# A transform of 64 by 32 points with half-array matmuls, and two bias rows added by matmul

## The reference

```python
# block 1: Hyena operator, order 2
proj = (layernorm(x) @ in_proj_w + in_proj_b).reshape(B, L, C, 3)
v = depthwise_conv3(proj[..., 0]) + short_b
h = gelu(gelu(pos @ fw1 + fb1) @ fw2 + fb2)
coefs = (h @ fw3 + fb3).reshape(L, C, 2)
for i in range(2):                       # only i = 1 reaches the output
    conv = irfft(rfft(v, 2L) * rfft(coefs[..., i], 2L), 2L)[:, :L]
    output = proj[..., i + 1] * conv
x = x + output @ out_w + out_b
# block 2: a weighted sum of 8 chosen adapters, one 512x512 matrix W and one bias b
x = x + layernorm(x) @ W.T + b
```

## Time and profile before

| | us |
|---|---|
| median of 3 runs (lowest, highest) | 2708.38 (2707.97, 2709.68) |
| span of the profiled execution; no other time of it is given | 2708.2 |
| busy: TensorE, VectorE, GpSimd, ScalarE | 2570.4, 1723.3, 1304.6, 1289.9 |

### The profile page before, as it was taken

One profiled execution on the slowest core, in us unless ns is written; L12 is line 12 of the kernel. 1 busy time (PEld: TensorE's weight loads), 2 busy tenths in 40 slices (PEclk: granted clock), 3 DMA queues, 4 the chain that ended last, 5 costly groups with the idle time before them and its releaser, 6 DMA issues. The chain is left out here.

```text
span 2708.2 us, 38386 instructions
## 1 busy us (share of the span) xinstructions
PE 2570.4 (95%) x11252; PEld 1859.0 (69%) x11252; DVE 1723.3 (64%) x2429; ACT 1289.9 (48%) x2021; POOL 1304.6 (48%) x1446
## 2 busy tenths in 40 slices
PE   7679999999999999799999997899999999999999
PEld 2268888888888888433333332788888888888887
DVE  5834434343443434477777776788888888888886
ACT  6634444444444444599999997222222222222222
POOL 1422222222222222366666664676767767776775
PEclk8889999999999999999999999999999999999999
DMA  6533443444344343777777776665555555555553
GB/s 207 171 121 117 183 167 132 158 155 159 119 180 170 128 164 139 263 248 259 263 254 252 249 252 227 233 212 171 169 165 170 170 161 172 169 165 170 169 166 124
DMA packets 233303, 495.89 MB, mean 183 GB/s; under 512 B 20299, under 2 KB 37004, under 8 KB 220244
## 3 DMA queue, kind: packets, MB, share of 16 engines
q1 hardware_dynamic: 181012, 394.39, 43.4%
q10 hardware_dynamic: 52224, 100.68, 9.9%
HBM read 275.58 MB, written 219.43 MB: 183 GB/s over the span
## 5 line engine op out<-in xcount | busy, mean ns | idle before, releaser
L1114 POOL TENSOR_TENSOR m_m<-m_zs,m_spec 128x512 f32<-128x512 f32 x256 | 345.2, 1353 | 240.7 <-ACT m_zs L1070 218.0
L776 POOL TENSOR_TENSOR vl<-v,vh 128x512 fp32r<-128x512 f32 x128 | 165.3, 1291 | 469.7 <-ACT vh L728 469.7
L1029 PE MATMUL m_psW<-m_u,mats 128*128 128x512 f32 x512 | 283.4, 636 | 48.8 <-DVE m_u L1143 48.1
L1143 DVE TENSOR_TENSOR m_u<-m_m 128x512 f32<-128x512 f32 x256 | 269.4, 1062 | 90.2 <-POOL m_m L1114 51.2
L1070 ACT ACTIVATE m_zs<-m_psZ 64x512 f32<-64x512 f32 x512 | 302.5, 591 | 22.1 <-DVE m_m L1131 9.1
L880 DVE COPY fs1o<-psS 128x512 f32<-128x512 f32 x128 | 88.5, 691 | 334.6 <-PE psS L201 334.6
L1305 ACT ACTIVATE b_z<-b_y,b_shift,b_rstd 128x512 f32<-128x512 f32 x128 | 104.3, 815 | 376.0 <-POOL b_shift L1269 376.0
L728 ACT ACTIVATE vh<-v 128x512 fp32r<-128x512 f32 x128 | 80.9, 632 | 401.7 <-DVE v L859 401.7
L1330 PEld LDWEIGHTS b_psC<-b_s,b_fin 128*128 128x128 f32 x2048 | 249.9, 193 | 23.6 <-DMA b_fin<-spec 12.9
L1330 PE MATMUL b_psC<-b_s,b_fin 128*128 128x128 f32 x2048 | 250.9, 276 | 12.5 <-DMA b_fin<-spec 12.5
L1018 PE MATMUL m_psZ<-m_xin,mats 128*128 128x512 f32 x512 | 256.7, 594 | 0.0
(11 more groups left out here) (128 smaller groups left out, 5894.4 us busy)
## 6 DMA issues: line engine op xcount, KB each, us to landing
m_xin<-spec SPq DMA_DIRECT2D x31, 2304.0 KB, 13.2
spec<-fs1o SPq DMA_DIRECT2D x64, 1024.0 KB, 5.8
spec<-m_wo ACTq DMA_DIRECT2D x64, 1024.0 KB, 7.0
b_fin<-spec SPq DMA_DIRECT2D x128, 512.0 KB, 3.7
xg<-in_L_attn_x_dram SPq DMA_DIRECT2D x32, 1024.0 KB, 4.8
gate_t<-gto SPq DMA_DIRECT2D x32, 1024.0 KB, 4.3
b_gin<-gate_t SPq DMA_DIRECT2D x128, 256.0 KB, 3.6
b_xin<-in_L_attn_x_dram SPq DMA_DIRECT2D x128, 256.0 KB, 3.8
```

The lines of the kernel that those rows point to most:

```text
L776: pool.tensor_tensor(vl[:, t % 2], v[:, t % 2], vh[:, t % 2].bitcast(F32), ALU.subtract).then_inc(v_lo, 1)
L1029: pe.matmul(psW[k][:], kind(INV, i, t), u[:, (t % GB - 1) % R, :], start=True, stop=True).then_inc(w_ps, 1)
L1114: pool.tensor_tensor(m2[:, b % R, :], zs[:, b % R, :], spec[:, par, 1, :], ALU.mult).then_inc(m2_done, 1)
L1143: dve.tensor_tensor(u[:, b % R, :], m1[:, b % R, :], m2[:, b % R, :], ALU.add).then_inc(u_done, 1)
```

## The change

All of the transform goes over to 64 by 32 points: 64 slots of spectrum instead of 128 and 32 inner indices. A tile is now two inner indices, t and t + 16, of 64 rows each (h = 0, 1), in partitions 0 to 63 and 64 to 127; there are 16 tiles per batch as before (`T`). The transform steps become pairs of matmuls on half of the array, without tile positions being named: they follow from the partitions of the operands.

- `prep`: filter rows, running sums and first transform in pairs; the channel-major filter, its copies, three scans and the rearrangements go; the sum runs over the hidden layer (one scan), and a second matmul chain (`sums`) turns it into edge rows.
- `front`: `stage1` has six matmuls on 64 rows each; the gate is projected row-major tile by tile (`project_g`), its bias added by VectorE; one copy of both banks on ScalarE.
- `middle`: weights hold each matrix beside its swapped form, so that a pair of row halves gives both parts of the product; one VectorE product of 1024 columns; the inverse is a pair of column halves and adds the two parts; swap, GpSimd's product and the sum go.
- `back`: `conv` is a pair of column halves with row-major result; `turn_o` transposes the gated rows; both bias rows enter as a first matmul on 64 rows in `project` and `adapt`; `bias_x` and `bias_y` go; lags and orders change.

```diff
 # front, TensorE
-                    for j in range(2):
-                        mm = mm3(pe, psS[j][:], s1h[:, t, j * P:(j + 1) * P], s1l[:, t, j * P:(j + 1) * P],
-                                 vh[:, t % 2], vl[:, t % 2], True, True)
+                    lo, hi = slice(0, N1), slice(N1, P)
+                    for half, h in ((lo, 0), (hi, 1)):
+                        pe.matmul(psS[:, h, :], s1h[half, t, :], vh[half, t % 2, :], start=True, stop=False)
+                    for half, h in ((lo, 0), (hi, 1)):
+                        pe.matmul(psS[:, h, :], s1h[half, t, :], vl[half, t % 2, :], start=False, stop=False)
+                    for half, h in ((lo, 0), (hi, 1)):
+                        mm = pe.matmul(psS[:, h, :], s1l[half, t, :], vh[half, t % 2, :], start=False, stop=True)
...
-                pipelined(pe, B, N2, [(turn, 2), (project_v, 3), (project_x2, 6), (stage1, 4)])
+                pipelined(pe, B, T, [(turn, 2), (project_v, 3), (project_g, 3), (stage1, 4)])
 # middle, TensorE
+            PAIR_AT = {0: 0, 2: 1, 4: 2, 7: 3}
...
-                    pe.matmul(psZ[(t % GB - 1) % R][:], kind(FWD, i, t), xin[:, par, t % GB - 1, :],
-                              start=True, stop=True).then_inc(z_ps, 1)
+                    pe.matmul(psA[k % RA][:, 0, :], w[0:R2], src[0:R2], start=True, stop=True)
+                    mm = pe.matmul(psA[k % RA][:, 1, :], w[R2:P], src[R2:P], start=True, stop=True)
...
-                    pe.matmul(psW[k][:], kind(INV, i, t), u[:, (t % GB - 1) % R, :], start=True, stop=True).then_inc(w_ps, 1)
+                    for k in range(2):
+                        pe.wait_ge(m_done, n + k + 1)
+                        pe.matmul(psW[0:R2, k, :], back_first if first else back_w, m[:, (2 * pair + k) % RM, 0, :], start=True, stop=True)
+                        pe.matmul(psW[R2:P, k, :], back_w, m[:, (2 * pair + k) % RM, 1, :], start=True, stop=True).then_inc(w_ps, 1)
 # middle, VectorE
+                    dve.tensor_tensor(m[:, (k - 1) % RM], psA[k % RA][:], spec[:, par], ALU.mult).then_inc(m_done, 1)
 # back, TensorE
-                    for ct in range(CT):
-                        for j in range(2):
-                            mm = pe.matmul(psC[t % 2][:, ct * P:(ct + 1) * P], fin[:, t % 2, j, ct * P:(ct + 1) * P],
-                                           s4[:, j, t, :], start=(j == 0), stop=(j == 1))
+                    for h in range(2):
+                        mm = pe.matmul(psC[t % 2][h * N1:(h + 1) * N1, :], s4[:, h * T + t, :], fin[:, t % 2, h, :], start=True, stop=True)
+                def turn_o(b, t):
+                    pe.wait_ge(o_done, no(b, t) + 1)
...
+                        mm = pe.transpose(psP[:, ct * P:(ct + 1) * P], o[:, t % 2, ct * P:(ct + 1) * P], ident[:])
                 def project(b, t):
...
+                    pe.matmul(psO[t % 2][:], share_r[:], bohl[:], start=True, stop=False)
...
                 def adapt(b, t):
...
+                    pe.matmul(psF[t % 2][:], share_r[:], bfhl[:], start=True, stop=False)
...
-                pipelined(pe, B, N2, [(conv, 1), (project, 2), (turn, 3), (adapt, 4)])
+                pipelined(pe, B, T, [(conv, 1), (adapt, 4), (turn_z, 3), (turn_o, 1), (project, 2)])
 # prep, TensorE: filter_rows, and sums likewise with cum and ramp_r
-                        pe.matmul(pA[e % 2][:], h2[:, cols], w3s[:], start=True, stop=False)
+                    for h in range(2):
+                        cols = h2[:, e + h * T:e + h * T + (N1 - 1) * N2 + 1:N2]
+                        pe.matmul(pA[e % 2][h * N1:(h + 1) * N1, :], cols, w3s[:], start=True, stop=False)
+                    pe.matmul(pA[e % 2][:], inside_r[:, where], b3hl[:], start=False, stop=True).then_inc(H_ps, 1)
```

More of the change, by code:

```diff
@@ L347, in _ @@
+                for i in range(4):
+                    sp.wait_ge(e0_stored[i], 16 * T // 4)
+                for i in range(3):
+                    sp.wait_ge(e1_stored[i], 16 * len(range(i, T, 3)))
+                sp.wait_ge(consts_in, 32)
                 sp.wait_ge(fc["x_in"][0], 16)
@@ new lines, in sums, with stage1 @@
+                def sums(t):
+                    if t >= 2:
+                        pe.wait_ge(e1_done, t - 1)
+                    for h in range(2):
+                        cols = cum[:, t + h * T:t + h * T + (N1 - 1) * N2 + 1:N2]
+                        pe.matmul(pE[t % 2][h * N1:(h + 1) * N1, :], cols, w3s[:], start=True, stop=False)
+                    pe.matmul(pE[t % 2][:], ramp_r[:, t * P:(t + 1) * P], b3hl[:], start=False, stop=True).then_inc(c_ps, 1)
+                def stage1(t):
+                    edge_row = t == T - 1
+                    pe.wait_ge(g_done, t + 1)
+                    if t >= 2:
+                        pe.wait_ge(s1_out, t - 1)
+                    for h in range(2):
+                        half = slice(h * N1, (h + 1) * N1)
+                        end = not (edge_row and h == 1)
+                        mm = pe.matmul(pS[t % 2][:, h, :], s1[half, t, :], g[half, t % GR, :], start=True, stop=end)
+                    if edge_row:
+                        pe.wait_ge(before_done, 1)
+                        mm = pe.matmul(pS[t % 2][:, 1, :], s1x[:], g_before[:], start=False, stop=True)
+                    mm.then_inc(s1_ps, 1)
@@ L501, in _ @@
+                for e in range(T + LAG):
+                    if e < T + 2:
+                        filter_rows(e)
+                    if e == 0:
+                        pe.wait_ge(cum_done, 1)
+                    if e < T:
+                        sums(e)
                     if e == LAG:
@@ L1145, in _ @@
-                pipelined(dve, GROUPS // 2, T, [(same_part, 0), (product, 2)])
+                    par, k = s // GB, s % GB
+                    n = data_no(i, s)
+                    dve.wait_ge(a_ps, n + 1)
+                    if k == 1:
+                        dve.wait_ge(f_done, group(i, s) + 1)
+                    if not (at_first(i, s) and k <= RM):
+                        dve.wait_ge(w_ps, n - RM + 1)
+                    dve.tensor_tensor(m[:, (k - 1) % RM], psA[k % RA][:], spec[:, par], ALU.mult).then_inc(m_done, 1)
```

833 lines of the change are left out of this document (352 added, 481 removed).

## The result

The changed kernel takes 3200.58 us (median of 4 runs, 3197.47 to 3203.96), the kernel before 2709.03 beside it: a ratio of 1.1816, 95% interval [1.1799, 1.1832]. Predicted were 2894 us and a range that ended at 3140. The direction was right; the size was not, and neither was the reason. The profiled execution spans 3202.1 us.

The account below looks back on a forecast made before the run. TensorE was taken to bound front and back, and a loop of ScalarE, VectorE and GpSimd middle. The sum was 2708 - 12 (prep) - 39 (front) + 60 (middle) + 177 (back) = 2894 us, range 2630 to 3140.

Parts of the forecast that it names:

- Prep, -12: Prep: copies, rearrangements and three scans go, half-array pairs come; 112 to 130 us against 137.8, taken as -12 us.
- Front, -39: Front: six whole matmuls become three pairs and two mode changes, -0.31 us a tile over 128 tiles, -39 us.
- Middle, +60: Middle: TensorE becomes the bound with 17 pairs, late second halves and mode changes; 19.6 us per group, 627 us, +60.
- but in program order: Fp32 pairs: the second half's first record starts only with the first half's second, so n pairs take 0.86 n + 0.43 us.
- rival 1: Whole kernel: pairs overlap wholly, mode changes still cost 0.19 us; middle -51, back +122, total 2728 us; chance 0.13.
- The term of 0.43 per run: Middle: a late second half at the end of each of eight runs per group, 8 x 0.43 = 3.4 us.
- Back, +177: Back: TensorE's tile goes from 7.81 to 9.19 us with bias matmuls, transposes and five mode changes, +177 us.
- The relief: Back: the two additions on VectorE and GpSimd were hidden by slack, so removing them brings nothing.
- the lower bound by the loop: Back: the chain from projection through y, statistics and z to the next projection needs 8.1 us per tile, +37 us.
- the late second halves: Middle and back: second halves start late; 0.43 us per run in middle, a lone pair in back 1.29 us, not 0.86.

Follow-up runs that it names:

- e_before_share: Kernel before with back's two bias additions replaced by matmuls over 64 rows, transform and transfers as before; 2861.20 us, ratio 1.0562.
- e_back16: Changed kernel with back's load of x and store of the output written as two transfers each, one per half; 2755.79 us, ratio 1.0177.
- e_adds16: Changed kernel with back's x load and output store in two transfers each, and both bias rows added by additions again; 2742.19 us, ratio 1.0116.
- e_turnz_rows128: Changed kernel with back's transfers split in two, bias matmuls on 128 rows, and z's transpose between adapter and projection; 2660.60 us, ratio 0.9817.
- e_adds: Changed kernel with both bias rows of back added by additions again, x's first in VectorE's order, slow transfers kept; 3317.44 us, ratio 1.2249.
- e_before2: Kernel before with back's x load and output store taken as a pattern of 2 x 64 rows; 3306.30 us, ratio 1.2205.
- e_x16: Changed kernel with back's load of x alone written as two transfers, the output store left as it was; 2775.58 us, ratio 1.0247.
- e_adds_late: Changed kernel with bias additions and slow transfers, b_out added to x right ahead of the addition that needs it; 3198.83 us, ratio 1.1815.

## Why the prediction was wrong

- **Prep, -12.** Too much: the first transpose of front starts at 144.3 us, for 143.8. In the other kernels with this prep it starts between 138.8 and 145.1, so the gain is 5 us at most and in most traces less. TensorE has 4 us less to do, but waits for `e`, which VectorE makes (21.5 us in ten waits), and VectorE for the store of `e` (12.4). Which of these sets the part was not tested.
- **Front, -39.** Right: its last stage-1 product starts at 1058.0 for 1095.4 us, 37 less; the tile is 7.07 us by its transposes (144.3 to 1042.8 over 127), for 7.09 predicted. With 0.23 for a pair of fp32r halves and 0.19 for a change the sum holds.
- **Middle, +60.** Wrong by its sign: -43 by the windows (524 for 567). The step was "but in program order": the second half's first record was to wait for the first half's second. It doesn't; pairs start 0.01 us apart. Without that term the same sum is rival 1's 516 us, and the first forward to the last inverse takes 515.9 (1071.3 to 1587.2). The term of 0.43 per run in eight runs of 32 groups was 110 us of forecast that did not exist. The argument took the order of the records from rows in which nothing could have overlapped. By the sentence of the Trainium skill on packs (TensorE: Matmul & The Clock Gate, Part 3) the prediction worked out 0.86 for a pair, and the trace of the changed kernel agrees.
- **Back, +177.** This is the step that failed. In TensorE's part only the pair was off, 0.86 us for 1.29. The changes were well priced: the bias matmuls with two changes each are 1.22 for 1.22 (`e_before_share`). In `e_back16` it is 2.08 us from the last matmul ahead of conv to the second one behind the bias matmul (2304.37 to 2306.45); 0.23, 0.86, 0.23 and 0.23 are 1.55, so three changes are 0.53 or 0.18 each, and column halves cost like row halves. But the transfers were weighed in middle alone, and there by bytes. Back's were put at nothing, without a reason; their bytes had not changed. The diff changed the order of two patterns, `n p c` to `h n t c`, and that set 12.17 us, 3.37 over the 8.80 of `e_back16`, in all 127 x 3.37 = 428 us, and 17 more at the end. Measured by mending it: 445.
- **The relief.** That the two additions "were hidden, and removing them brings nothing" holds in the kernel before: without them the bias matmuls cost their full 1.22 us a tile. And the lower bound by the loop, 8.1 us a tile, was real: it is what kept `e_adds16` from gaining, and it is part of `e_back16`. Three changes at 0.18 added to the 8.10 of `e_turnz_rows128` give an estimate of 8.65 for TensorE alone; the other 0.15 of the 8.80 is then the wait for z. That rival 1 had 8.76 is in part luck.

Does the sum close? 2894 less the late second halves (110 in middle, 55 in back) is 2729, rival 1's sum but for rounding. The profiled execution of `e_back16` spans 2750.2 us, 42 more than the kernel before, where rival 1 had 20. Between marks that both traces have (front's first transpose, its last stage-1 product, the last inverse of middle, the end) the differences are -4.6, -36.0, -52.7 and +135.3 us; rival 1 had -12, -39, -51 and +122. Of the 13 in back, 10 are its tile, 1.04 us longer (8.80 for 7.76) and not 0.95 (8.76 for 7.81), and 3 its start and end. The transfers add 445. Rival 1 had a chance of 0.13; no rival had the transfers, and no bound of the range took them in.

What stays open: what sets prep's time, and why `e_adds` lets the two engines run dry and `e_before2` does not.

## What to carry to other kernels

Price every transfer that a diff touches by its pattern, not its bytes: look at the slowest dimension of both sides, divide the packets by the engines that it can use, and add what else those engines carry in the same tile. The signs in a profile are transfers that land late at a low DMA share, a rate that keeps returning to one low figure, and long issues on a queue. And where a loop of small operations is as long as a tile, place each step where it is covered: the same instructions took 8.63, 8.28 and 7.67 us a tile in three orders.

## What was not expected of the hardware

- Two fp32 matmuls on disjoint rows, or columns, interleave record by record: 0.86 us for the pair, 1.71 for two on the same rows.
- A load and a store of 128 rows of 2048 bytes, each written as 2 x 64 rows, ran at 51 GB/s in all, two of sixteen DMA engines by the busy share, and shared the pair; a transfer of 128 x 2 rows beside them landed after 21.7 us for 3.7.
- TensorE's mean granted clock in back was 0.89 of 2.4 GHz in the changed kernel, where TensorE stood for 355 of 1601 us, and 0.85 to 0.90 from 2000 to 2400 us in the other kernels whose transfers set the tile. In that window it was 1.00 in the nine kernels with mended transfers (in `e_x16` the load alone). It is not what made back slow: the changed kernel at 0.90 and `e_adds_late` at 0.86 have 12.17 and 12.13 us a tile.
